# First expert layer: products turned and projected down in pairs of tiles, with the last 48 channels of the two tiles in different halves of the partitions

## The reference

```
scores = softmax(xt @ Wg.T)                       # 16 experts in 4 groups
topi   = top 4 experts out of the 2 best groups   # combine: their scores as weights
h          = silu(xt @ W1[e].T) * (xt @ W3[e].T)  # 176 inner channels
expert_out = h @ W2[e].T                          # back to 256 channels
y = sum over the 4 chosen experts of weight * expert_out
z = silu(xt @ Ws1.T) * (xt @ Ws3.T) @ Ws2.T       # two shared experts
out = y + z
```

## Time and profile before

| | |
|---|---|
| median of 3 runs | 1257.81 us (1256.96 to 1258.76) |
| the profiled execution, its own time | 1256.46 us |
| its span, first to last instruction | 1254.6 us |
| mean granted TensorE clock | 0.966 of full |
| busy share of TensorE, VectorE, ScalarE, GpSimd | 89%, 40%, 41%, 34% |
| the 79 tiles of the first expert layer | from about 416 to 623 us of the span |

### The profile page before, as it was taken

How to read it: one execution, slowest core, us unless ns; L and a number is a source line. 1 busy time by engine, 2 the same in 40 slices (tenths; PEclk the granted TensorE clock), 3 DMA queues, 4 the chain that set the end, 5 groups by cost and what they waited for, 6 DMA issues and landing times. The chain is left out here.

```text
span 1254.6 us, 29167 instructions
## 1 busy us (share of the span) xinstructions
PE 1121.8 (89%) x10346; PEld 873.0 (70%) x10347; DVE 496.1 (40%) x1265; ACT 511.9 (41%) x1291; POOL 423.5 (34%) x541
## 2 busy tenths in 40 slices
PE   5889898999889899999977888887848999999997
PEld 2567676776555677777655676776627989999997
DVE  1235464555374133233255666665276000000332
ACT  1423545434533333333235555555413434333332
POOL 2023021031136886778434443211124200100443
PEclk8999999999999999999988999998968999999999
DMA  6049809021065455655281110000026655555672
GB/s 191 18 141 357 301 24 351 32 70 60 18 266 131 161 191 163 186 158 155 80 319 36 35 36 19 19 18 2 2 102 226 226 164 173 184 190 171 206 255 85
DMA packets 116521, 173.18 MB, mean 138 GB/s; under 512 B 17440, under 2 KB 94096, under 8 KB 114960
## 3 DMA queue, kind: packets, MB, share of 16 engines
q1 hardware_dynamic: 89936, 128.46, 31.4%
q0 software_dynamic: 9696, 26.75, 6.5%
q10 hardware_dynamic: 16784, 16.49, 4.0%
HBM read 105.07 MB, written 65.27 MB: 136 GB/s over the span
## 5 line engine op out<-in xcount | busy, mean ns | idle before, releaser
L2564 PE MATMUL bank<-m_XGT,m_w 128*128 128x128 f32 x1248 | 148.3, 278 | 0.0
L2564 PEld LDWEIGHTS bank<-m_XGT,m_w 128*128 128x128 f32 x1248 | 145.2, 195 | 1.2 <-issue 1.0
L2578 PE MATMUL bank<-w,m_HT 128*128 x624 | 141.0, 379 | 0.0
L2578 PEld LDWEIGHTS bank<-w,m_HT 128*128 128x128 f32 x624 | 115.7, 190 | 14.1
L2396 ACT ACTIVATE m_HT<-bank,m_b 128x128 f32<-128x128 f32 x312 | 89.2, 368 | 80.9 <-PE bank L2564 80.9
L1598 PE MATMUL bank<-m_W,m_XGT 128*128 x316 | 107.3, 462 | 0.6 <-ACT m_XGT L1455 0.6
L1455 ACT ACTIVATE m_XGT<-bank 128x256 f32<-128x256 f32 x79 | 30.3, 384 | 122.4 <-DVE m_US L1542 111.7
L2356 POOL DMA_INDIRECT m_GA<-ys,r_pos x32 | 31.4, 982 | 133.2 <-SPq L2311 124.5
L1212 POOL DMA_INDIRECT GA<-ys,r_pos x64 | 64.5, 1007 | 31.4 <-issue 16.5
L1534 DVE TENSOR_TENSOR m_H<-bank,m_SG 128x176 f32<-128x176 f32 x79 | 26.9, 341 | 117.5 <-ACT m_SG L1459 117.5
L1392 POOL DMA_INDIRECT xs<-X,r_pos x64 | 63.3, 989 | 27.7 <-issue 14.0
(11 more groups left out here) (368 smaller groups left out, 2344.2 us busy)
## 6 DMA issues: line engine op xcount, KB each, us to landing
m_w<-in_m_w SPq DMA_DIRECT2D x35, 1024.0 KB, 5.3
xs<-zeros SPq DMA_DIRECT2D x1, 10112.0 KB, 33.7
ys<-zeros SPq DMA_DIRECT2D x1, 10112.0 KB, 35.2
ys<-m_US ACTq DMA_DIRECT2D x79, 128.0 KB
m_GS<-xs SPq DMA_DIRECT2D x72, 128.0 KB
w<-in_m_w SPq DMA_DIRECT2D x8, 1024.0 KB, 15.8
m_W<-in_w SPq DMA_DIRECT2D x2, 2816.0 KB, 13.5
xs<-zeros SPq DMA_DIRECT2D x1, 4992.0 KB, 19.4
```

The costliest lines, as they stand in the source:

```text
L2564: last = nc.tensor.matmul(BU[i][:, c * P:(c + 1) * P], w1[:, b, m, lo:lo + P], XGT[:, b % 2, m * P:(m + 1) * P], start=m == 0, stop=m == K ...
L2578: last = nc.tensor.matmul(BY[b % 2][:, 0:DIM], HT[:, b % 2, c, :], w2[:, bass.ds(e, 1), c, :], start=c == 0, stop=c == CH - 1)
```

## The change

TensorE now works on two tiles at a time (`pair_pipeline`: the same loop with two tiles in a step). A step does gate and up of tiles j+2 and j+3, turns the rows of j+4 and j+5, projects tiles j and j+1 down, and turns the products of j+2 and j+3. VectorE writes the last 48 channels of an even tile into columns 0 to 47 of a common third block of `H`, those of an odd tile into columns 64 to 111, in a second instruction. So three transposes turn the products of both tiles, and one ScalarE copy takes all three out of PSUM. Behind the transposes the 48 channels lie on partitions 0 to 47 and 64 to 111. The even tile takes its weights from `W2B`, the odd tile from a new buffer `odd` of two slots, into which SyncE loads 48 rows of W2 for each odd tile. The zero fill of `W2B` goes, and GpSimd clears one block of `H` in place of `HT`. The visits of VectorE stay behind tiles 56 and 68.

```diff
+def pair_pipeline(engine, step, n, visits=(), done=0):
+    for at, visit in (*visits, (n - PEEL, None)):
+        with engine.Fori(done // 4, at // 4) as i:
+            for b in range(0, 4, 2):
+                step(i * 4 + b, b, None)
+        if visit:
+            visit()
+        done = at
+    for j in range(n - PEEL, n, 2):
+        step(j, j % 4, n - 1 - j)
...
-                sp.dma_start(W2B[KI:P], fx.zeros[KI:P].unsqueeze(1).broadcast_to([P - KI, E0, DIM])).then_inc(ld_w, 16)
+                def load_odd(e, b):
+                    sp.dma_start(odd[HALF:HALF + KI, b // 2].unsqueeze(1),
+                                 io["w2"][P:I0, bass.ds(e, 1), :]).then_inc(ld_odd[b // 2], 16)
...
                 def load(j, b, checked=None):
+                    if b % 2:
+                        e = expert(j - BEHIND)
...
                     sp.wait_ge(t_full, j + 1)
+                    if b % 2:
+                        load_odd(e, (b - BEHIND) % 4)
...
+                for j in range(NT - BEHIND, NT - 1, 2):
+                    e = expert(j)
+                    sp.wait_ge(y_full, j - 3)
+                    load_odd(e, j % 4)
...
-                nc.gpsimd.memset(HT, 0.0).then_inc(padded, 1)
+                nc.gpsimd.memset(H[:, 2, :], 0.0).then_inc(padded, 1)
...
+                def turned_pair(j):
+                    act.wait_ge(ht_full, j + 2)
+                    nc.scalar.activation(HT[:, 0:3, :].rearrange("p c t -> p (c t)"), BH[0][:, 0:3 * P],
+                                         ACT.Copy).then_inc(ht_used, 2)
...
                 def product(j, b):
                     dve.wait_ge(gate, j + 1)
-                    nc.vector.tensor_tensor(H[:, b % 2, :], BU[b % 2][:, I0:IW], SG[:, b % 2, :],
+                    at = HALF * (b % 2)
+                    nc.vector.tensor_tensor(H[:, b % 2, :], BU[b % 2][:, I0:I0 + P], SG[:, b % 2, 0:P], ALU.mult)
+                    nc.vector.tensor_tensor(H[:, 2, at:at + KI], BU[b % 2][:, I0 + P:IW], SG[:, b % 2, P:I0],
                                             ALU.mult).then_inc(h_done, 1)
...
+                def turn_pair(j, ahead):
+                    pe.wait_ge(h_done, j + (2 if follows(ahead, 3) else 1))
+                    nc.tensor.transpose(BH[0][:, 0:P], H[:, 0, :], fx.ident[:])
+                    if follows(ahead, 3):
+                        nc.tensor.transpose(BH[0][:, P:2 * P], H[:, 1, :], fx.ident[:])
+                    nc.tensor.transpose(BH[0][:, 2 * P:3 * P], H[:, 2, :], fx.ident[:]).then_inc(ht_full, 2)
+
+                def down_pair(j, b, both, first):
+                    e = [expert(j + k) for k in range(2 if both else 1)]
+                    if not first:
+                        pe.wait_ge(y_used, j)
+                    pe.wait_ge(ht_used, j + 2)
+                    if both:
+                        pe.wait_ge(ld_odd[b // 2], 4 * (j - b) + 16)
+                    for k in range(len(e)):
+                        nc.tensor.matmul(BY[k][:, 0:DIM], HT[:, k, :], W2A[:, bass.ds(e[k], 1), :],
+                                         start=True, stop=False)
+                    nc.tensor.matmul(BY[0][:, 0:DIM], HT[0:KI, 2, :], W2B[0:KI, bass.ds(e[0], 1), :],
+                                     start=False, stop=True).then_inc(y_full, 1)
+                    if both:
+                        nc.tensor.matmul(BY[1][:, 0:DIM], HT[HALF:HALF + KI, 2, :], odd[HALF:HALF + KI, b // 2, :],
+                                         start=False, stop=True).then_inc(y_full, 1)
+
+                def step(j, b, ahead, first=False):
+                    for k in (2, 3):
+                        if follows(ahead, k):
+                            gate_up(j + k, b + k)
+                    for k in (4, 5):
+                        if follows(ahead, k):
+                            rows(j + k, (b + k) % 4)
+                    down_pair(j, b, follows(ahead, 1), first)
+                    if follows(ahead, 2):
+                        turn_pair(j + 2, ahead)
```

More of the change, by code:

```diff
@@ L1283, in moe0 @@
     NT = fx.NS0
-    IW, KI = 2 * I0, I0 - P
+    IW, KI, HALF = 2 * I0, I0 - P, P // 2
     POOL_GATES = 2 * SC
-    FIRST, CHECKED = 7, 32
+    FIRST, CHECKED, BEHIND = 7, 32, 6
     with ExitStack() as mem:
@@ L1295, in moe0 @@
         W13 = sb("W13", [P, KC, E0, IW])
-        W2A, W2B = sb("W2A", [P, E0, DIM]), sb("W2B", [P, E0, DIM])
+        W2A, W2B, odd = sb("W2A", [P, E0, DIM]), sb("W2B", [P, E0, DIM]), sb("odd", [P, 2, DIM])
         S13, S2 = fx.S13, fx.S2
@@ L1313, in moe0 @@
         ht_full, ht_used = sem("ht_full"), sem("ht_used")
+        ld_odd = [sem(f"ld_odd{b}") for b in range(2)]
         y_full, y_used = sem("y_full"), sem("y_used")
@@ L1471, in step @@
                 def step(j, b, ahead):
-                    if follows(ahead, 3):
-                        rows(j + 3, b + 3)
                     if follows(ahead, 2):
                         silu(j + 2, b + 2)
-                    if follows(ahead, 1):
-                        turned_product(j + 1, b + 1)
-                    store(j, b)
+                    if follows(ahead, 3):
+                        silu(j + 3, b + 3)
+                    for k in (4, 5):
+                        if follows(ahead, k):
+                            rows(j + k, b + k)
+                    if follows(ahead, 2):
+                        turned_pair(j + 2)
+                    for k in range(2):
+                        if follows(ahead, k):
+                            store(j + k, b + k)
                 def load(j, b):
@@ L1500, in _ @@
                 shared_rows(PAIRS - 1)
+                silu(1, 1)
                 rows(2, 2)
                 load(6, 2)
-                silu(1, 1)
-                turned_product(0, 0)
-                tile_pipeline(act, step, NT)
+                rows(3, 3)
+                turned_pair(0)
+                pair_pipeline(act, step, NT)
             @block.vector
@@ L1533, in product, with result @@
                     dve.wait_ge(gate, j + 1)
-                    nc.vector.tensor_tensor(H[:, b % 2, :], BU[b % 2][:, I0:IW], SG[:, b % 2, :],
+                    at = HALF * (b % 2)
+                    nc.vector.tensor_tensor(H[:, b % 2, :], BU[b % 2][:, I0:I0 + P], SG[:, b % 2, 0:P], ALU.mult)
+                    nc.vector.tensor_tensor(H[:, 2, at:at + KI], BU[b % 2][:, I0 + P:IW], SG[:, b % 2, P:I0],
                                             ALU.mult).then_inc(h_done, 1)
-                def step(j, b, ahead):
-                    if follows(ahead, 2):
-                        product(j + 2, b + 2)
+                def result(j, b):
                     dve.wait_ge(y_full, j + 1)
@@ L1542, in step @@
                     nc.vector.tensor_copy(Y[:, b % 2, :], BY[b % 2][:, 0:DIM]).then_inc(y_used, 1)
+                def step(j, b, ahead):
+                    for k in (2, 3):
+                        if follows(ahead, k):
+                            product(j + k, b + k)
+                    for k in range(2):
+                        if follows(ahead, k):
+                            result(j + k, b + k)
+                dve.wait_ge(padded, 2)
                 product(0, 0)
                 product(1, 1)
-                tile_pipeline(dve, step, NT, ((56, lambda: fx.l1.moments_on_dve(nc, dve, fx.X, r.steps)),
+                pair_pipeline(dve, step, NT, ((56, lambda: fx.l1.moments_on_dve(nc, dve, fx.X, r.steps)),
                                               (68, lambda: fx.l1.apply_on_dve(nc, dve, fx.X))))
@@ L1627, in _ @@
                 pe.wait_ge(r.placed, 3)
-                pe.wait_ge(ld_w, 80)
+                pe.wait_ge(ld_w, 64)
                 gate_up(0, 0)
                 shared_down(GROUPS - 1, (1,))
+                gate_up(1, 1)
                 rows(2, 2)
-                gate_up(1, 1)
-                turn_product(0, 0)
+                rows(3, 3)
+                turn_pair(0, None)
                 pe.wait_ge(z_used, PAIRS)
-                tile_pipeline(pe, step, NT)
+                step(0, 0, None, True)
+                step(2, 2, None)
+                pair_pipeline(pe, step, NT, done=4)
                 busy(nc, BH[0], fx.ones[:], 5)
```

28 lines of the change are left out of this document (4 added, 24 removed).

## The result

The changed kernel takes 1270.65 us (median of 4 runs, 1269.72 to 1274.42) against 1257.38 (4 runs, 1255.83 to 1258.76) for the kernel before: ratio 1.0112, 95% interval 1.0088 to 1.0135. It is 13.3 us slower. The forecast was 1256.0, with a range up to 1261.0.

A forecast was written before the change was run, and what follows sets the result against it. TensorE, full in the expert layer, bounds it except where VectorE's visit waits for GpSimd's chain. After that wait 599.8 + 19.2 + 1.7 + 0.4 = 621.1 against 622.93, -1.8 us, giving 1256.0 us; range 1251.5 to 1261.0.

The forecast's parts named there:

- The transposes and the overlap of the short halves: TensorE, per pair: three transposes for four, -0.11 us; four short W2B passes cost as two, -0.43 us.
- the rival of half the overlap: TensorE's short W2B passes: in strict order only one of two overlaps, 4.97 us a pair, 1256.9 us; chance 0.10.
- Changing the shape, +0.31: TensorE, switching to the short products' array shape once a pair: costs 0.31 us, low bound 0.
- Waits of the new order: The pair's transposes wait for VectorE's second product; claimed covered by about 1 us of TensorE's other work.
- the forecast's own number for the pair: TensorE's time for a pair of tiles: 4.75 us against 4.98, -0.23 us.
- something else on the path slows: Rival: GpSimd's chain above all slows, or the odd load comes late in each pair, to 1260 us; chance 0.10.
- the slower rival: TensorE's short halves run one after the other and the shape change is paid: +0.20 us a pair, 1262.0 us; chance 0.12.
- The odd tile's load: SyncE's load of 48 W2 rows: 3.9 us available; behind next-layer weights perhaps a microsecond or two late, swallowed before 598.
- GpSimd's chain anchors the visit: VectorE's visit behind tile 68 waits for GpSimd until about 598; TensorE's 7.9 us gain before it becomes waiting, leaving -1.8 us.
- the signs named for it: At the visit: VectorE idle some 11 us, released by GpSimd at 597.3 to 598.1; TensorE idle about 10 us, then low clock.
- both signs of being wrong: VectorE's idle at the visit under 6 us, or GpSimd's L1270 ending before 596 or after 599.
- The end, 621.1: TensorE's last work of the stage: 599.8 + 19.2 + 1.7 + 0.4 = 621.1 against 622.93, -1.8 us.

The follow-up runs named there:

- e4_halves_apart: Changed kernel with down products in tile order, long and short of the first tile, then of the second; ratio to the kernel before 1.0212, pairs of 5.71 us.
- e1_kept: Changed kernel, but down products take expert numbers from registers that gate and up of the same tile loaded; pairs of 4.89 us, ratio to the kernel before 1.001.
- e5_early: As e1_kept, with the loads for the next step's two gate/ups ahead of the wait for the products; ratio to the kernel before 0.9978, pairs of 4.78 us.
- b3_side_edits: Kernel before, one tile at a time, with kept and early expert-number loads and next-layer weight loads split over four places; no gain, pairs of 4.98 us.
- e10_visit60: Changed kernel with kept and early expert-number loads, split weight loads, and VectorE's second visit behind tile 60 instead of 68; ratio to the kernel before 1.0129.

## Why the prediction was wrong

- *The transposes and the overlap of the short halves:* right. The start of the second product is 0.01 us behind the first, as named, and the passes start even, odd, even, odd, though the program has the even tile's product first. So the rival of half the overlap falls. The Trainium skill, "TensorE: Matmul & The Clock Gate", Part 3, says that matmuls start and end in strict order; taken pass by pass in the order of the program the trace doesn't agree, since the odd tile's first pass starts 0.31 us before the even tile's second (559.26 and 559.57).
- *Changing the shape, +0.31:* right in size. 0.09 late before the first pass, 0.20 in the two passes, 0.05 in the transposes behind, 0.34 in sum. The pair is 4.78 where nothing holds it (4.75 said). The other price in that part, 0.39 for the second change in e4_halves_apart, is near it.
- *"Waits of the new order", the pair's transposes wait for the second product, "covered by about 1 us":* this step failed. The sum had the array at 4.75 us a pair, and pairs took 5.45. The cover was counted for the array alone, and for it even 0.6 us was enough (product 564.06, transposes 564.67). What I didn't ask is what stands in TensorE's queue behind the waiting instruction. The step says it for the odd load only ("the pair's down products"), and the loads of expert numbers and the loop's branch are in no term of the sum. Taking two of the four loads of a pair and the checks away (e1_kept) gave 0.53 us a pair back, moving the others (e5_early) another 0.11, and with that the forecast's own number for the pair stands. No rival had it; the rival "something else on the path slows" named GpSimd and the odd load, and the slower rival put its price on the halves, whose overlap held.
- *The odd tile's load "may come late, by a microsecond or two", "before 598 and is swallowed there":* the size was off. A wait of 1.9 us in the changed kernel, where slow pairs left time, but 6.4 us where pairs run at 4.78. With late placing nothing behind it swallows it.
- *Where the gain goes, GpSimd's chain anchors the visit:* the signs named for it didn't appear, and both signs of being wrong did (VectorE without idle time there, root at 599.4, later than 599), since TensorE came 10 us late. The mechanism itself is right and shown, in b3_side_edits and e10_visit60. The 7.9 us for its 34 pairs are 7.8 by their own terms; nothing hangs on it.
- *The end, 621.1:* it was 634.5. The tail from there also missed 1.8 us of filling products at the lower clock.

## What to carry to other kernels

Before two steps are joined, write down the queue of each engine, register loads and branches with it, and ask what stands behind each wait, not only what the wait holds up. Loads that need nothing from the wait belong ahead of it, a number already loaded belongs in a register, and a check that goes with each load is to be counted with it. A gain then meets the next fixed time of another engine (here a root on GpSimd, and a row of seven weight loads on SyncE); those places are to be moved with it.

## What was not expected of the hardware

- A load into a register with a check of its bounds takes TensorE's queue 0.65 us from start to start: 0.36 the load (its record is 0.30, now and then up to 0.71), 0.29 the check. A loop's branch takes 0.5 us (564.11 to the next load at 564.61).
- "issue" as the releaser can mean that the queue was late, with the array idle: 7.4 and 4.7 us by the matmuls of two lines here.
- Two products on 48 partitions in different halves, written to two banks, run at the same time, 0.64 us for both.
- The same kernel on the same chip took 1257 us in one batch and 1292 in another; the traces show the difference as waits for placed token tiles.
